# Latent attention: the order of key products, score tiles and the value sum within a step of TensorE

## The chip, the cores and the metric

One NeuronCore of a Trainium2 chip runs the whole program. The metric is the device time of one execution in microseconds, as the median of several runs.

## The reference

A decoder of two layers on x (2 x 1024 tokens, 256 channels). Each layer adds a self attention, a cross attention and a feed-forward block, each on the normalised x. Only the first block matters here, the latent attention of layer 0 (16 heads of 16 channels):

```python
latent_kv = (k + v) @ W_down_kv
k_rec, v_rec = latent_kv @ W_up_k, latent_kv @ W_up_v
scores = jnp.einsum('bhqd,bhkd->bhqk', qh, kh) * scale
decay = jnp.exp(-LAMBDA_DECAY * TIME_STEP * jnp.abs(idx[:, None] - idx[None, :]))
scores = scores * decay[None, None, :, :]
attn = jax.nn.softmax(scores, axis=-1)
out = jnp.einsum('bhqk,bhkd->bhqd', attn, vh)
```

(Clips, reshapes and the output projection are left out.) The softmax runs over all 1024 keys of a batch.

## The kernel before

The function `latent_attention` works in 16 groups of four heads and 512 queries (GROUPS), two groups for each set of heads. The products of queries and keys are needed twice, and are computed twice. First come the *score tiles* (`scores`, matmuls of line 653): 128 queries against 1024 keys of one head, 16 tiles a group, each in two of the PSUM banks 0 to 3. VectorE multiplies such a tile by the decay inside the diagonal block and takes each query's largest score (`highest`, line 814). When the 16 tiles of a group have been taken, GpSimd splits the peaks into three bf16 parts (`split_peaks`, lines 758 to 764), TensorE turns them into rows (`turn_peaks`, line 709), ScalarE copies the rows (`copy_peaks`, line 918) and SyncE stores them beside the stacked queries (line 623). So the peak is taken off within the matmul when the products come a second time: the *key products* (`key_scores`, line 660), 128 keys against 512 queries of one head, keys on the partitions, one bank each. ScalarE takes the exponential of each (`exponential`, line 913). In every second step the diagonal block has a *diagonal unit* of its own (`diagonal_scores`, four small matmuls, line 660 as well), and GpSimd selects the right side of the two (`select`, lines 772 and 775). The *value sum* (`sum_values`, lines 698 and 701) multiplies the probabilities of one key tile with the values of four heads in f32, four heads side by side in the columns of the array, and adds up in bank 7. When a group's eight key tiles are summed, ScalarE copies the sum (`copy_mix`, line 924), TensorE turns it (`turn_mix`, line 718), and VectorE divides by the sum of the weights (`weight`, lines 796 and 798).

A group has eight steps i, one for each key tile. What is interleaved in a step on TensorE is written out by hand in the loop of lines 725 to 739: the value sum of two steps ago, two key products, a score tile of the next group (tiles run ahead by LEAD = 6), two key products, a score tile; then `turn_peaks` of the next group if i is 5 (TURN_STEP), the diagonal unit if i is odd, `turn_mix` of the group before if i is 3. The score tiles end with step 4 of group 14, as then all groups have theirs.

Key products, the diagonal unit, and the results of both turns share three banks, 4 to 6, in a ring. The list `ring` holds all users in their order, each with the semaphore and the count that free it; `wait_for_bank` makes a user wait for the one three places ahead of it. For a key product that is its exponential; for `turn_mix` it is the weighting of its group by VectorE; for `turn_peaks` the copy of the rows. A score tile waits for VectorE to have taken the tile two before it (`peaked`).

VectorE has its own hand-written order (`run`, line 818), which must name tiles, units and weightings in TensorE's order. On the path without clips, which the profiled execution takes, a unit's step does nothing (`lambda g, i, h: None`), so VectorE's order is two tiles a step and, behind those of step 3, the weighting of the group before. ScalarE's queue has four exponentials a step, the mix copy of the group before behind the first one of step 1, the copy of the peak rows behind the fourth of step 5, and the diagonal unit's exponential at the end of odd steps.

Of the kernel before, what the change touches and what calls it, by code (L numbers as in the profile page):

```python
# [504 lines left out]
HEADS = 4  # L505
# [32 lines left out]
def latent_attention(k, v_heads, attn, decay, inner, stacks):  # L538
# [9 lines left out]
    GROUPS = 2 * B * H // HEADS  # L548
    TILES = HEADS * TPG
    LEAD = 6  # L550
    TURN_STEP = 5
# [6 lines left out]
    def on_diagonal(i):  # L558
        return i % 2 == 1

    def unit_index(g, i, h):

        return g * UNITS + i * HEADS + i // 2 + h
# [4 lines left out]
    def block_of(g, i):  # L568
        return key_tile(g, i) - g % 2 * TPG
# [17 lines left out]
    def bank_of(item):  # L587
        return 4 + place[item] % 3

    def wait_for_bank(pe, item):  # L590

        if place[item] >= 3:
            pe.wait_ge(*ring[place[item] - 3])

    with ExitStack() as c, nc.Block() as block:
# [16 lines left out]
        def tile_at(g, i, x):  # L612

            return (g + 1) * TILES + 2 * i + LEAD + x
# [25 lines left out]
        def _(pe):  # L640
            def scores(tile):

                g, x = divmod(tile, TILES)
                h, j = divmod(x, TPG)
                if x == 0:
                    stacks_arrived(pe, stacks, g)
                wait(pe, peaked, tile - 1)
                edge = (g % 2 * TPG + j + 1) * P
                for version in range(2):
                    for half in range(2):  # L650
                        lo, hi = max(half * G, 0 if version == 0 else edge), min((half + 1) * G, edge if version == 0 else S)
                        if lo < hi:
                            last = pe.matmul(k.ps[:, 2 * (tile % 2) + half, lo - half * G:hi - half * G],  # L653
                                             stacks.q[0:ROWS, g % 3, version, h, j * P:(j + 1) * P],
                                             stacks.k[0:ROWS, g // 2 % 2, version, h, lo:hi], start=True, stop=True)
                last.then_inc(scored, 1)

            def key_product(g, i, h, bank, version, lo, hi, at):
                kt = key_tile(g, i)
                return pe.matmul(k.ps[:, bank, at:at + hi - lo],  # L660
                                 stacks.k[0:ROWS + PARTS, g // 2 % 2, version, h, kt * P:(kt + 1) * P],
                                 stacks.q[0:ROWS + PARTS, g % 3, version, h, lo:hi], start=True, stop=True)

            def key_scores(g, i, h):

                item = (exp_done, unit_index(g, i, h) + 1)
                if i == 0 and h == 0:
                    pe.wait_ge(peaks_in, (g + 1) * 16)
                wait_for_bank(pe, item)
                edge = min(max(block_of(g, i) * P, 0), G)  # L670
                if edge > 0:
                    last = key_product(g, i, h, bank_of(item), 1, 0, edge, 0)
                if edge < G:
                    last = key_product(g, i, h, bank_of(item), 0, edge, G, edge)
                last.then_inc(key_scored, 1)

            def diagonal_scores(g, i):

                item = (exp_done, unit_index(g, i, HEADS) + 1)
                wait_for_bank(pe, item)  # L680
                lo = block_of(g, i) * P
                for h in range(HEADS):
                    last = key_product(g, i, h, bank_of(item), 1, lo, lo + P, h * P)
                last.then_inc(key_scored, 1)

            def sum_values(s):

                g, i = divmod(s, QT)
                n, kt = g // 2, key_tile(g, i)
                pe.wait_ge(exp_done, unit_index(g, i, HEADS if on_diagonal(i) else HEADS - 1) + 1)  # L690
                if i == 0:
                    pe.wait_ge(v_staged, n + 1)
                    wait(pe, mix_copied, g)
                if on_diagonal(i):
                    pe.wait_ge(selected, s // 2 + 1)
                    lo = block_of(g, i) * P
                    for h in range(HEADS):
                        pe.matmul(k.ps[VW * h:VW * (h + 1), PV_BANK, lo:lo + P], vh[:, n % 2, h, kt, :],
                                  probs_d[:, s // 2 % 2, h, :], start=False, stop=False, skip_group_check=True)
                for h in range(HEADS):  # L700
                    last = pe.matmul(k.ps[VW * h:VW * (h + 1), PV_BANK, :], vh[:, n % 2, h, kt, :], probs_of(s)[:, h, :],  # L701
                                     start=i == 0, stop=i == QT - 1, skip_group_check=True)
                last.then_inc(summed, 1)

            def turn_peaks(g):
                item = (peaks_copied, g + 1)
                pe.wait_ge(peaks_split, g + 1)
                wait_for_bank(pe, item)
                pe.matmul(k.ps[0:PARTS * 2 * TILES, bank_of(item), 0:P],
                          peak_parts[:, g % 2, :, :, :].rearrange("p r v t -> p (r v t)"),  # L710
                          ident_b[:, :], start=True, stop=True).then_inc(peaks_turned, 1)

            def turn_mix(g):
                item = (weighted, g + 1)
                pe.wait_ge(mix_copied, g + 1)
                wait_for_bank(pe, item)
                for j in range(TPG):
                    last = pe.transpose(k.ps[:, bank_of(item), j * P:(j + 1) * P], mix[:, g % 2, j * P:(j + 1) * P], k.ident[:, :])
                last.then_inc(mix_turned, 1)
# [4 lines left out]
                    turn_peaks(0)  # L724
            for g in range(GROUPS):
                for i in range(QT):
                    if g * QT + i >= 2:
                        sum_values(g * QT + i - 2)
                    for x in range(2):
                        for h in range(2 * x, 2 * x + 2):  # L730
                            key_scores(g, i, h)
                        if tile_at(g, i, x) < GROUPS * TILES:
                            scores(tile_at(g, i, x))
                    if i == TURN_STEP and g + 1 < GROUPS:
                        turn_peaks(g + 1)
                    if on_diagonal(i):
                        diagonal_scores(g, i)
                    if i == 3 and g > 0:
                        turn_mix(g - 1)
            for s in range(GROUPS * QT - 2, GROUPS * QT):  # L740
# [49 lines left out]
        def _(dve):  # L790
            def weight(g):
                b, first = divmod(g // 2 * HEADS, H)
                t = b * QT + g % 2 * TPG
                o = k.ps[:, bank_of((weighted, g + 1)), :].rearrange("p (j h d) -> p j h d", h=HEADS, d=VW)
                dve.wait_ge(mix_turned, g + 1)
                dve.reciprocal(inv[:, g % 2, :, :], o[:, :, :, HD]).then_inc(inverted, 1)
                dve.wait_ge(inverted, g + 1)
                dve.tensor_tensor(attn[:, t:t + TPG, first * HD:(first + HEADS) * HD].rearrange("p j (h d) -> p j h d", d=HD),
                                  o[:, :, :, 0:HD], inv[:, g % 2, :, :].unsqueeze(3).to_broadcast([P, TPG, HEADS, HD]),
                                  ALU.mult).then_inc(weighted, 1)  # L800
# [17 lines left out]
            def run(tile_step, unit_step, group_step):  # L818
                for tile in range(TILES + LEAD):
                    tile_step(tile)  # L820
                for g in range(GROUPS):
                    group_step(g)
                    for i in range(QT):
                        for x in range(2):
                            for h in range(2 * x, 2 * x + 2):
                                unit_step(g, i, h)
                            if tile_at(g, i, x) < GROUPS * TILES:
                                tile_step(tile_at(g, i, x))
                        if on_diagonal(i):
                            unit_step(g, i, HEADS)  # L830
                        if i == 3 and g > 0:
                            weight(g - 1)
                weight(GROUPS - 1)

            def clipped_path():
# [53 lines left out]

                own.did(dve.nop(nofuse=True))  # L890
                run(clipped_highest, clip_unit, spread_peaks)

            inside = dve.value_load(k.inside[0:1, 0:1], min_val=0, max_val=1)
# [1547 lines left out]
```

## Time and profile before

| | |
|---|---|
| median of three runs | 1449.26 us (1446.63 to 1449.71) |
| the profiled execution | 1447.3 us |
| its span | 1445.6 us |
| TensorE busy (matmul) | 1223.4 us, 85% of the span |
| VectorE, ScalarE busy | 798.4 and 763.2 us |

The latent attention's steps run from about 110 to 525 us of the span. All times in the rows further down are microseconds from the span's start. A row of the order of time merges instructions of one line that follow each other on an engine: start, length up to the last one's end, engine, line, operation, output and inputs, how many, and in brackets how long the engine had been idle and what ended that. Matmuls overlap in the array, so a row's length reaches past the next row's start; what a piece costs is the distance from its start to the next start. PE is TensorE's matmul, PEld its weight load, DVE VectorE, ACT ScalarE, POOL GpSimd.

### The profile page before, as it was taken

How to read it: one execution, taken by the hardware profiler on the slowest of the kernel's cores; microseconds unless marked ns; L12 is line 12 of the kernel's file. 1: busy time of each engine (PE TensorE's matmuls, PEld its weight loads, DVE VectorE, ACT ScalarE, POOL GpSimd, SP SyncE). 2: the span in 40 equal slices, each digit the busy share in tenths (PEclk: the TensorE clock that was granted, in tenths of full speed). 3: DMA queues.
4: the chain of work that ended last, by engine and by line, in shares of the span. 5: the costliest groups of instructions: out<-in, count | busy, mean ns of one | idle time of the engine just before them, and what ended most of it. 6: DMA issues, size and time to landing. Idle time of an engine off the chain costs nothing. (4 is left out here: it accounts for less than half of the span.)

```text
span 1445.6 us, 25437 instructions
## 1 busy us (share of the span) xinstructions
PE 1223.4 (85%) x8789; PEld 729.6 (50%) x8790; DVE 798.4 (55%) x1729; ACT 763.2 (53%) x1456; POOL 331.5 (23%) x567
## 2 busy tenths in 40 slices
PE   4869999999999987988456999878883799999992
PEld 2313444444444355435125552554362699999991
DVE  6977777777777427235777544572346322222223
ACT  3826777777777742663675668424632233333330
POOL 2922222222222211143520000211131222222220
PEclk9959999999999999999558999999996799999996
DMA  6770213321330003000001000051037111111115
GB/s 213 250 220 24 68 38 76 68 69 44 81 76 25 2 2 97 1 2 8 15 0 35 1 1 1 5 213 61 2 97 233 29 37 36 36 36 36 36 30 182
DMA packets 58656, 89.85 MB, mean 62 GB/s; under 512 B 10330, under 2 KB 48372, under 8 KB 56884
## 3 DMA queue, kind: packets, MB, share of 16 engines
q1 hardware_dynamic: 52694, 76.19, 17.7%
q0 software_dynamic: 3744, 10.23, 2.3%
q10 hardware_dynamic: 2112, 2.10, 0.4%
q8 instruction: 58, 0.95, 0.3%
q14 instruction: 48, 0.39, 0.1%
HBM read 66.21 MB, written 21.89 MB: 61 GB/s over the span
## 5 line engine op out<-in xcount | busy, mean ns | idle before, releaser
L814 DVE CUSTOM_DVE_ANT_0 faded_scores_sb<-banks,inner_sb 128x1024 f32<-128x1024 f32 x256 | 303.3, 1222 | 92.5 <-PE banks L653 91.4
L913 ACT ACTIVATE xt_sb<-banks 128x512 f32<-128x512 f32 x344 | 179.0, 605 | 72.2 <-PE banks L660 72.2
L660 PE MATMUL banks<-q_stack_sb,k_stack_sb 99*128 99x128 bf16 (+3 forms) x960 | 180.4, 296 | 5.9 <-ACT xt_sb L913 2.6
L653 PE MATMUL banks<-k_stack_sb,q_stack_sb 96*128 96x512 bf16 (+3 forms) x704 | 163.4, 338 | 7.2 <-DVE peak_sb L814 4.0
L660 PEld LDWEIGHTS banks<-q_stack_sb,k_stack_sb 99*128 99x128 bf16 x960 | 70.4, 97 | 159.9 <-ACT xt_sb L913 66.9
L2121 PEld LDWEIGHTS banks<-slots_xt_sb,attn_sb 128*128 128x128 f32 x1248 | 146.6, 193 | 1.9
L2121 PE MATMUL banks<-slots_xt_sb,attn_sb 128*128 128x128 f32 x1248 | 146.7, 276 | 0.0
L2133 PE MATMUL banks<-experts_w_sb,xt_sb 128*128 x624 | 141.2, 379 | 1.3 <-issue 1.3
L2133 PEld LDWEIGHTS banks<-experts_w_sb,xt_sb 128*128 128x128 f32 x624 | 115.5, 190 | 15.8 <-issue 1.7
L2173 ACT ACTIVATE slots_xt_sb<-banks 128x256 f32<-128x256 f32 x39 | 14.9, 383 | 177.5 <-PE banks L2107 177.5
L2230 DVE TENSOR_TENSOR slots_y_sb<-banks,tile_b_sb 128x256 f32<-128x256 f32 x39 | 16.6, 425 | 166.3 <-PE banks L2133 166.3
L913 ACT ACTIVATE probs_sb<-banks 128x512 f32<-128x512 f32 x168 | 87.3, 605 | 34.0 <-PE banks L660 34.0
L653 PEld LDWEIGHTS banks<-k_stack_sb,q_stack_sb 96*128 96x128 bf16 x704 | 65.8, 100 | 69.0 <-DVE peak_sb L814 17.9
L1227 DVE TENSOR_REDUCE peak_sb<-banks 128x8 f32<-128x616 f32 x64 | 49.9, 797 | 85.7 <-PE banks L1062 85.7
L701 PE MATMUL banks<-xt_sb,v_head_sb 128*32 128x512 f32 x688 | 90.6, 598 | 0.0
L252 POOL TENSOR_TENSOR x_sb<-x_sb,bb_sb 128x256 f32<-128x256 f32 x48 | 33.0, 731 | 244.9 <-DMA bb_sb<-in_L_attn_bo 193.8
L2183 ACT ACTIVATE xt_sb<-banks,tile_b_sb 128x128 f32<-128x128 f32 x312 | 84.7, 386 | 8.3 <-PE banks L2121 6.7
L1274 ACT ACTIVATE pt_sb<-banks,keyfill_sb 77x1024 f32<-77x1024 f32 x64 | 67.5, 1104 | 34.4 <-PE banks L1093 33.5
L2214 DVE COPY attn_sb<-experts_w_sb 128x2048 f32 x39 | 48.0, 1230 | 42.5 <-PE banks L2121 27.9
L2163 POOL DMA_INDIRECT outputs_y<-slots_y_sb,output_row_sb x39 | 39.6, 1015 | 127.5 <-DVE slots_y_sb L2230 127.5
L772 POOL TENSOR_SCALAR_AFFINE_SELECT xt_sb<-xt_sb 128x512 f32<-128x512 f32 x43 | 27.3, 635 | 180.8 <-ACT xt_sb L913 180.8
L2154 POOL DMA_INDIRECT slots_x_sb<-tokens_x,token_sb x39 | 38.2, 980 | 96.9 <-PE banks L2107 86.2
(316 smaller groups left out, 2017.0 us busy)
## 6 DMA issues: line engine op xcount, KB each, us to landing
experts_w_sb<-in_L_ffn_W SPq DMA_DIRECT2D x16, 1024.0 KB, 11.9
k_stack_sb<-k_parts SPq DMA_DIRECT2D x48, 256.0 KB, 4.9
q_stack_sb<-q_parts SPq DMA_DIRECT2D x96, 128.0 KB, 3.4
q_parts<-parts_sb SPq DMA_DIRECT2D x16, 384.0 KB, 2.6
k_parts<-parts_sb SPq DMA_DIRECT2D x16, 384.0 KB, 3.9
xt_sb<-outputs_y SPq DMA_DIRECT2D x8, 512.0 KB, 6.7
x_sb<-in_x SPq DMA_DIRECT2D x4, 512.0 KB, 5.6
w_raw_sb<-in_w_t SPq DMA_DIRECT2D x2, 1024.0 KB, 6.2
```

Of the source, the lines that this page charges most:

```text
L653: last = pe.matmul(k.ps[:, 2 * (tile % 2) + half, lo - half * G:hi - half * G], stacks.q[0:ROWS, g % 3, version, h, j * P:(j + 1) * P], st ...
L660: return pe.matmul(k.ps[:, bank, at:at + hi - lo], stacks.k[0:ROWS + PARTS, g // 2 % 2, version, h, kt * P:(kt + 1) * P], stacks.q[0:ROWS ...
L701: last = pe.matmul(k.ps[VW * h:VW * (h + 1), PV_BANK, :], vh[:, n % 2, h, kt, :], probs_of(s)[:, h, :], start=i == 0, stop=i == QT - 1, sk ...
L814: dve.tensor_tensor_reduce(out=junk[:, tile % 2, :], in0=tile_scores(tile), in1=inner[:, window(tile)], scale=1.0, scalar=-3.0e38, op0=ALU ...
L913: act.activation(out, k.ps[:, bank_of((exp_done, u + 1)), :], ACT.Exp).then_inc(exp_done, 1)
L1227: dve.tensor_reduce(peak[:, t % TPG, 2 * half:2 * half + 2, :], k.ps[:, bank:bank + 2, 0:SLOTS * C].rearrange("p r (s n) -> p r s n", n=C) ...
L1274: act.activation(pt[:, n % 2, 2 * half:2 * half + 2, :], k.ps[0:C, 2 * half:2 * half + 2, :], ACT.Exp, bias=key_fill[:, b:b + 1]).then_inc ...
L2121: last = pe.matmul(k.ps[:, 2 * u + f // HALF, (f % HALF) * P:(f % HALF + 1) * P], w1[:, u, kd, f * P:(f + 1) * P], xst[:, u, kd, :], start ...
L2133: last = pe.matmul(k.ps[:, 6, s * D:(s + 1) * D], ht[:, s, f, :], r.w2[:, bass.ds(e, 1), f, :].rearrange("p a n -> p (a n)"), start=f == 0 ...
L2163: pool.indirect_dma_start(out=scratch.y[:, :], out_offset=bass.IndirectOffsetOnAxis(ap=r.row[:, n:n + 1], axis=0), in_=ys[:, n % 2, :], in ...
L2183: ins = act.activation(ht[:, s, f, :], k.ps[:, 2 * s + f // HALF, (f % HALF) * P:(f % HALF + 1) * P], ACT.Gelu_apprx_tanh, bias=b1[:, s, f ...
L2214: dve.tensor_copy(w1[:, u, :, :].rearrange("p k n -> p (k n)"), r.w1[:, bass.ds(e, 1), :, :].rearrange("p a k n -> p (a k n)")).then_inc(c ...
```

## The change

The value sum moves behind the first two key products of a step. The third key product comes next, then the first score tile, then the fourth key product. `turn_peaks` (step 5) and the diagonal unit (odd steps) follow it directly, ahead of the second score tile, which is now the last of the step but for `turn_mix`. VectorE's order names the units and tiles in the same order.

```diff
             for g in range(GROUPS):
                 for i in range(QT):
+                    for h in range(2):
+                        key_scores(g, i, h)
                     if g * QT + i >= 2:
                         sum_values(g * QT + i - 2)
                     for x in range(2):
-                        for h in range(2 * x, 2 * x + 2):
-                            key_scores(g, i, h)
+                        key_scores(g, i, 2 + x)
+                        if x == 1:
+                            if i == TURN_STEP and g + 1 < GROUPS:
+                                turn_peaks(g + 1)
+                            if on_diagonal(i):
+                                diagonal_scores(g, i)
                         if tile_at(g, i, x) < GROUPS * TILES:
                             scores(tile_at(g, i, x))
-                    if i == TURN_STEP and g + 1 < GROUPS:
-                        turn_peaks(g + 1)
-                    if on_diagonal(i):
-                        diagonal_scores(g, i)
                     if i == 3 and g > 0:
                         turn_mix(g - 1)
...
                     for i in range(QT):
+                        for h in range(2):
+                            unit_step(g, i, h)
                         for x in range(2):
-                            for h in range(2 * x, 2 * x + 2):
-                                unit_step(g, i, h)
+                            unit_step(g, i, 2 + x)
+                            if x == 1 and on_diagonal(i):
+                                unit_step(g, i, HEADS)
                             if tile_at(g, i, x) < GROUPS * TILES:
                                 tile_step(tile_at(g, i, x))
-                        if on_diagonal(i):
-                            unit_step(g, i, HEADS)
                         if i == 3 and g > 0:
                             weight(g - 1)
```

## Rows read from the trace of the kernel before

**Rows 1.** Busy by stretch: length, engines' busy us, PEclk, DMA share, GB/s.

```profile
120.00:490.00 370.00, 367.45 (x2947) 151.79 (x2945) 281.40 (x488) 274.56 (x547) 87.01 (x181) 1.00 0.23 56
496.00:515.00 19.00, 16.50 (x132) 5.41 (x132) 0.68 (x2) 15.52 (x31) 3.89 (x7) 1.00 0.00 1
552.00:555.40 3.40, 3.40 (x18) 3.27 (x17) 3.29 (x12) 1.10 (x3) 0.00 (x0) 0.50 0.71 195
```

**Rows 2.** Order of time, TensorE: the value sums V(3) to V(7), V(0) to V(2).

```profile
300.06 0.43 PE L698 MATMUL banks<-probs_d_sb,v_head_sb 128*32 128x128 f32 x8
...
303.98 1.06 PE L701 MATMUL banks<-xt_sb,v_head_sb 128*32 128x512 f32 x8
...
306.82 0.43 PE L698 MATMUL banks<-probs_d_sb,v_head_sb 128*32 128x128 f32 x8
...
310.42 1.06 PE L701 MATMUL banks<-xt_sb,v_head_sb 128*32 128x512 f32 x8
...
313.26 0.42 PE L698 MATMUL banks<-probs_d_sb,v_head_sb 128*32 128x128 f32 x8
...
316.55 1.07 PE L701 MATMUL banks<-probs_sb,v_head_sb 128*32 128x512 f32 x8
...
319.38 0.42 PE L698 MATMUL banks<-probs_d_sb,v_head_sb 128*32 128x128 f32 x8
...
322.99 1.06 PE L701 MATMUL banks<-xt_sb,v_head_sb 128*32 128x512 f32 x8
```

**Rows 3.** Order of time, all engines: step 1 of a group, V(1) to D(1).

```profile
319.63 1.04 PE L701 MATMUL banks<-xt_sb,v_head_sb 128*32 128x512 f32 x8
...
320.60 0.11 PEld L660 LDWEIGHTS banks<-q_stack_sb,k_stack_sb 99*128 99x128 bf16 x2 [0.84 <-ACT xt_sb L913]
320.60 0.60 PE L660 MATMUL banks<-q_stack_sb,k_stack_sb 99*128 99x512 bf16 x2
...
321.03 0.60 ACT L913 ACTIVATE probs_sb<-banks 128x512 f32<-128x512 f32 x1 [0.99 <-PE banks L660]
...
321.52 0.59 ACT L924 ACTIVATE mix_sb<-banks 128x512 f32<-128x512 f32 x1
...
322.00 1.59 ACT L913 ACTIVATE probs_sb<-banks 128x512 f32<-128x512 f32 x3
322.66 0.23 PEld L660 LDWEIGHTS banks<-q_stack_sb,k_stack_sb 99*128 99x128 bf16 x4 [0.43 <-ACT probs_sb L913]
```

**Rows 4.** Order of time, all engines: S0(3), K0(4), weighting, S0(4), K2(4).

```profile
301.72 0.60 PE L653 MATMUL banks<-k_stack_sb,q_stack_sb 96*128 96x128 bf16 x3
...
304.98 0.60 PE L660 MATMUL banks<-q_stack_sb,k_stack_sb 99*128 99x512 bf16 x2
305.08 0.42 DVE L798 TENSOR_TENSOR attn_sb<-banks,inv_sb 128x256 f32<-128x256 f32 x1
...
305.42 0.60 PE L653 MATMUL banks<-k_stack_sb,q_stack_sb 96*128 96x384 bf16 x3
...
305.86 0.60 PE L660 MATMUL banks<-q_stack_sb,k_stack_sb 99*128 99x512 bf16 x2
```

**Rows 5.** Order of time, all engines: S0(4) and S1(4) on VectorE to D(5).

```profile
306.20 1.22 DVE L814 CUSTOM_DVE_ANT_0 faded_scores_sb<-banks,inner_sb 128x1024 f32<-128x1024 f32 x1 [0.69 <-PE banks L653]
...
307.35 1.22 DVE L814 CUSTOM_DVE_ANT_0 faded_scores_sb<-banks,inner_sb 128x1024 f32<-128x1024 f32 x1
...
308.46 2.06 ACT L913 ACTIVATE xt_sb<-banks 128x512 f32<-128x512 f32 x4 [0.99 <-PE banks L660]
...
309.36 0.60 PE L653 MATMUL banks<-k_stack_sb,q_stack_sb 96*128 96x512 bf16 x3
309.53 0.24 POOL L764 TENSOR_TENSOR peak_parts_sb<-peak_rest_sb,peak_parts_sb 128x32 bf16<-128x32 f32 x1
...
309.83 0.26 PE L709 MATMUL banks<-ident_b_sb,peak_parts_sb 128*96 128x128 bf16 x1
310.09 0.40 PE L660 MATMUL banks<-q_stack_sb,k_stack_sb 99*128 99x128 bf16 x4
```

## The prediction

> **What bounds the kernel now.** I read the page first for the engines and the granted clock, then the stretch of the latent attention alone, then the order of time of two steps, and last the places where TensorE starts something later than its own work allows. The change touches one stage only. In its 370 us from 120 to 490, TensorE is busy for 367.45 us at a granted clock of 1.00 (2.4 GHz), VectorE for 281 and ScalarE for 275 [rows 1]. So TensorE is the bound and the others have a quarter of their time free. But a busy TensorE can hide small waits, because the ends of matmuls are modelled, so I take the distances between starts.
>
> I call a step's pieces K0 to K3 (the key products, line 660), S0 and S1 (the two score tiles, 653), D (the diagonal unit, 660 x4), V (the value sum, 698 and 701), M (turn_mix, 718) and T (turn_peaks, 709). A number behind it in brackets is the step i of the group. From the starts [rows 2 to 4]: two K take 0.44, so one takes 0.22; an S takes 0.44; V takes 1.00 in an even step and 1.22 where line 698 comes with it; from D(1) to the V behind it are 0.33. An even step V to V is 2.84, and 1.00 + 4 x 0.22 + 2 x 0.44 is 2.76, with the rounding 0.09 over: what it costs to go over from bf16 products to V. So D is 0.33 - 0.09, or 0.23 rounded down. An odd step is 3.29, as step 7 shows: 1.22 + 0.88 + 0.88 + 0.23 + 0.09.
>
> The other step lengths [rows 2] tell where the order costs something now: step 3 takes 3.92, so M costs 0.63; step 5 takes 3.60, which is 0.31 over 3.29 (T and what waits about it); step 1 takes 3.61, 0.32 over. That last is a real wait: the mix copy stands in ScalarE's queue at 321.52 between two exponentials, and D(1) needs the bank of exp1 [rows 3]. The group is 2.84 x 4 + 3.29 + 3.92 + 3.60 + 3.61 = 25.8 us.
>
> **What the change does, part by part.** Nothing is added and nothing removed. TensorE's nominal work stays: V still follows bf16 work and is still followed by K, once a step, so the two changes of format stay too. On VectorE the order of real work is the same: its run takes the unmasked path (the custom operation of line 814 [rows 5]), on which the steps of units do nothing, so it still takes two tiles and, in step 3, the weighting. The list of banks has the order K0 K1 K2 K3 T D M before and after, so every wait has the value that it had. SyncE, GpSimd and ScalarE keep their queues. All that moves is *when*, within a step, TensorE comes to each wait. So I go through the waits.
>
> *K3 on exp0.* An exponential starts 0.43 after its product's start, lasts 0.60, and lets go some 0.06 later: 1.09 [rows 3]. K3 now comes 0.66 + 0.44 = 1.10 behind K0, just in time. It will come 1.09 + 0.22 + 0.44 later still. That is worth nothing where score tiles lie between. Where the tiles have run out (the last eleven steps), K3 waits 1.09 - 0.66 = 0.43 now; afterwards K1 waits for the exponential of the K2 or K3 three starts ahead of it, again 1.09 - 0.66. Nothing gained; I take 0, with 0.2 a step as bound on both sides, 2 us in all.
>
> *Step 1, the mix copy.* It waits for the last value sum of the group before, which is V(1). Count from V(1). V ends at 1.29 (319.63 + 1.04 less 319.38 [rows 2, 3]); the copy can start at about 1.34, exp1 at 0.48 behind it (1.82), and it lets go at 1.82 + 0.60 + 0.06 = 2.48. Now two key products, a tile and two more lie behind V and all that is waited for is D. Then D comes at 1.22 + 0.22 + 0.44 + 0.22 = 2.10 and waits 0.38. ScalarE goes on with exp2 at 2.30 and exp3 at 2.78, which lets go at 3.44; K1(2) comes at 2.48 + 0.23 + 0.44 + 0.22 = 3.37 and waits 0.07. V(2) is at 3.75 against 3.61: **+0.14**. Bounds: 0 (the copy starts as V's last pass ends) and 0.25.
>
> *Step 4, the weighting.* K2(4) takes the bank that M used, which VectorE frees with the weighting. VectorE can't do it earlier: in step 3 it has two tiles back to back. Now the weighting ends at 305.50, 3.78 behind S0(3), and K2(4) starts 4.14 behind it, so nothing waits [rows 4]. In the new order K2(4) is reached after S0 0.44, K3 0.22, D 0.23, S1 0.44, M 0.63, K0 and K1 0.44, V with its entry 1.09: 3.49. It must wait until 3.84: **+0.35**. Bounds: 0.2 (M dearer behind a tile than behind D) and 0.45.
>
> *Step 5, the turn of the peaks.* This is the dear one. T needs the peaks of the last tile of the next group, S1(4). The chain is: S0(4) at 305.42; VectorE takes it at 306.20 and S1(4) right behind at 307.35 (so S1's own time does not matter); GpSimd's four operations end at 309.77; T starts at 309.83, 4.41 behind S0(4) [rows 4, 5]. S1(5) had started at 309.36, so T waits 0.05 or less now: the chain is exactly covered. The new order puts T ahead of S1(5) and moves S0(4) later in its step as well. T is reached after S0(4) 0.44, K3 0.22, S1 0.44, K0 and K1 0.44, V with entry 0.09 + 1.22, K2 0.22, S0 0.44, K3 0.22: 3.73. It waits 0.68. In return D(5), which now starts 0.26 behind T because it waits for exp2 of its step (the third of the four in the row at 308.46, over at about 310.04), finds its bank free and follows at 0.06. Step 5 from V to V: 1.22 + 0.88 + 0.68 + 0.06 + 0.23 + 0.44 + 0.44 + 0.09 = 4.04 against 3.60: **+0.44**. Since K2(4) stands ahead of S0(4), its wait moves the whole chain and saves nothing here. Bounds: 0.25 and 0.6.
>
> *What could be late next.* T 0.4 later in the group brings the peak rows 0.8 nearer to the K0 of the next group that reads them: 6.9 us instead of 7.7, for one transfer; no row shows its landing, but no step 0 waits. I take 0; if that cover were gone it could cost up to 0.8 a group. The D of an odd step is ready long before; K1 behind it needs exp3 1.09 after K3 and comes 0.22 + 0.23 + 0.44 + 0.22 = 1.11 after: exactly enough, 0 to 0.03. S1 needs the banks of the step before's S1, off VectorE 0.78 + 1.15 x 2 = 3.1 behind that step's S0, and comes 2.84 + 0.66 = 3.5 behind it.
>
> **The sum.** The whole set of waits is in groups 1 to 13: 0.14 + 0.35 + 0.44 = 0.93 each, 12.1 us. Group 0 has no mix: 0.44. Group 14 has 0.49 and, without tiles behind T, about 0.1 in step 5. Group 15 has 0.14 in step 1, and in step 3 M runs beside exponentials that are waited for anyway: an estimate of -0.3. Together 12.9 us. The profiled execution took 1447.3 us (span 1445.6), 2.0 under the median of the three runs, 1449.26, and within their 1446.63 to 1449.71. So 1460.2 by the profile and 1462.2 by the median; I say 1461.
>
> **The rivals.**
> (1) *Weights loaded under V* (faster, 0.04). V costs 1.22 - 1.00 = 0.22 for 128 columns of each head, so 512 should cost 0.88 and not 1.00; 0.12 on leaving and 0.09 on entering are weight loads that nothing covers, 0.21 a step. The load of K0 behind V starts at 320.60, with its matmul, after 0.84 idle [rows 3]. If the new neighbours (K1 before, K2 behind, whose banks have been free for a microsecond) let these loads run ahead, 126 times 0.21 are 26 us back: 1461 - 26 = 1435. It decides from the first step without a wait. Against it: K0's bank was free as long, and it was late all the same.
> The Trainium skill, TensorE: Matmul & The Clock Gate, Part 2, step by step, says that the engine pulls weight loads ahead of running matmuls if their rows do not conflict or the spare weight buffer takes them. By that rule 1435 would be near; the trace agrees between K and S, and not behind V.
> (2) *The chain under T is shorter than I count* (no change, 0.05). If VectorE's two tiles or GpSimd's four operations took 0.7 less, T and the weighting would stay covered, and D(5) and D(1) decide: 1447 to 1450. The rows give no place for it.
> (3) *Half the waits* (0.03): 1455, if V's last pass and the weighting let go earlier than they end.
> (4) *The clock falls* (0.03). A stretch of 3.4 us at the lower level (0.50, 1.2 GHz) stands at 552 [rows 1]; in it TensorE does half its work, 1.7 us lost. One in each of 15 groups: +26, 1487. Against it: in the last steps, with TensorE busy 16.5 of 19 us, the clock stays at 1.00, and in the new order it will be busy for more than that.
> The same page, section on the second failure mode, says that small pauses between groups of matmuls that cycle through banks can make the clock swing. By it 1487 or more; the trace has such pauses in every group and shows no swing.
>
> **How the numbers follow.** Forecast 0.85, rivals 0.04, 0.05, 0.03, 0.03. The range takes the bounds of the three terms (0.45 to 1.3 a group, of which I leave out the outer quarters: 9 to 16 us), the 2 us of the last steps and the spread of the runs: 1455 to 1467. About 0.2%, 3 us, is what can be told from no change. Faster 0.04, same 0.05, slower 0.91.
>
> **What would show it.** In the new profile: steps of 4.04 (5), about 3.2 for V(4) to V(5), 3.75 (1), the rest as before; T held by GpSimd's line 764 for 0.7; a key product held by VectorE's line 798 in step 4. If T isn't held, the largest term is wrong; if even steps are shorter than 2.84, rival 1; if the clock row of the stage has anything but full, rival 4.

## The result, and the profile after

The changed kernel takes 1461.70 us (median of four runs, 1458.85 to 1462.95) against 1448.06 for the kernel before (four runs by now, 1446.63 to 1449.71): the ratio is 1.009, with a 95% interval of 1.0076 to 1.0105. It is slower by 13.6 us. The profiled executions took 1462.7 and 1447.3 us, with spans of 1460.9 and 1445.6.

The shortest view of where it went is the list of one line's instructions. The turn of the peaks T (line 709) comes once a group; the row gives how many there are, the shortest, median and longest in ns, and the first and last start in us. First the kernel before:

```profile
L709 PE MATMUL banks<-ident_b_sb,peak_parts_sb x16: 256/257/339, 107.0 to 490.2; 128*96 128x128 bf16 x16
```

and the changed kernel:

```profile
L709 PE MATMUL banks<-ident_b_sb,peak_parts_sb x16: 256/257/340, 107.3 to 505.8; 128*96 128x128 bf16 x16
```

From the first T to the last are 383.2 us before and 398.5 after. That is +15.3 us in 15 groups, 1.02 each. Ahead of the first T lie 107.0 and 107.3 us, behind the last 955.4 and 955.1: the sum of all the rest hardly moved. I use this distance, "T to T", for the runs below.

It needs a caution. The first T stands among the score tiles ahead of the first step, where the clock is low: from 105 to 115 us the granted clock is 0.50 in both kernels, from 115 to 125 us it is 0.99 before and 0.90 after. So T to T also holds what an edit puts behind the first T, and a piece at half speed. From the second T on the clock is full. In the same view from 120 us on, the second T starts at 129.5 us before and at 130.5 after, so from the second T to the last are 360.7 and 375.3 us: +14.6 in 14 groups, 1.04 each. Where an edit moves T to another step or changes the tiles that run ahead, only this second distance compares; a table further down has it for every run.

The busy time in nearly the same stretch as [rows 1], the changed kernel:

```profile
120.00:504.00 384.00, 367.05 (x2948) 153.84 (x2946) 283.69 (x488) 296.98 (x545) 86.88 (x177) 1.00 0.22 54
```

TensorE has done its 2948 matmuls with the same busy time (367.05 against 367.45 us for 2947), at the same full clock, but in 384 us instead of 370. The new time is waiting, not work. Who waited for whom, from 150 to 450, of the changed kernel (us in total, how many times, the longest):

```profile
PEld banks L660 <- DVE attn_sb L800: 16.3, 12, 1.4
...
PEld banks L709 <- POOL peak_parts_sb L766: 8.9, 11, 0.8
...
PE banks L709 <- POOL peak_parts_sb L766: 5.8, 11, 0.5
PE banks L660 <- DVE attn_sb L800: 5.5, 12, 0.5
```

In the same view of the kernel before TensorE's matmuls waited for nobody, and the weight loads of line 709 waited 2.5 us in all. Now a key product waits for VectorE's weighting (line 800) and T for GpSimd's last operation (line 766), once a group each. The steps, as the starts of the value sum V(1) to V(7), V(0) and V(1), in the order of time on TensorE:

```profile
301.56 0.43 PE L698 MATMUL banks<-probs_d_sb,v_head_sb 128*32 128x128 f32 x8
...
305.35 1.06 PE L701 MATMUL banks<-probs_sb,v_head_sb 128*32 128x512 f32 x8
...
308.19 0.43 PE L698 MATMUL banks<-probs_d_sb,v_head_sb 128*32 128x128 f32 x8
...
311.95 1.07 PE L701 MATMUL banks<-xt_sb,v_head_sb 128*32 128x512 f32 x8
...
315.32 0.43 PE L698 MATMUL banks<-probs_d_sb,v_head_sb 128*32 128x128 f32 x8
...
319.39 1.07 PE L701 MATMUL banks<-xt_sb,v_head_sb 128*32 128x512 f32 x8
...
322.23 0.43 PE L698 MATMUL banks<-probs_d_sb,v_head_sb 128*32 128x128 f32 x8
...
325.52 1.06 PE L701 MATMUL banks<-probs_sb,v_head_sb 128*32 128x512 f32 x8
...
328.36 0.43 PE L698 MATMUL banks<-probs_d_sb,v_head_sb 128*32 128x128 f32 x8
```

| step i, V to V, us | 1 | 2 | 3 | 4 | 5 | 6 | 7 | 0 | group |
|---|---|---|---|---|---|---|---|---|---|
| before [rows 2] | 3.61 | 2.84 | 3.92 | 2.84 | 3.60 | 2.84 | 3.29 | 2.84 | 25.8 |
| forecast | 3.75 | 2.84 | 3.92 | 3.19 | 4.04 | 2.84 | 3.29 | 2.84 | 26.7 |
| after | 3.79 | 2.84 | 3.76 | 3.37 | 4.07 | 2.84 | 3.29 | 2.84 | 26.8 |

And the two waits themselves in the order of time of all engines. The rows answer to those of [rows 4, 5]:

```profile
309.64 0.60 PE L653 MATMUL banks<-k_stack_sb,q_stack_sb 96*128 96x128 bf16 x3
...
310.51 0.60 PE L653 MATMUL banks<-k_stack_sb,q_stack_sb 96*128 96x256 bf16 x3
310.74 0.58 PEld L718 LDWEIGHTS banks<-ident_sb,mix_sb 128*128 128x128 f32 x4
310.95 0.60 PE L718 MATMUL banks<-ident_sb,mix_sb 128*128 128x128 f32 x4
...
312.99 0.42 DVE L800 TENSOR_TENSOR attn_sb<-banks,inv_sb 128x256 f32<-128x256 f32 x1
313.47 0.10 PEld L660 LDWEIGHTS banks<-q_stack_sb,k_stack_sb 99*128 99x128 bf16 x1 [1.36 <-DVE attn_sb L800]
313.47 0.39 PE L660 MATMUL banks<-q_stack_sb,k_stack_sb 99*128 99x512 bf16 x1 [0.45 <-DVE attn_sb L800]
...
313.70 0.60 PE L653 MATMUL banks<-k_stack_sb,q_stack_sb 96*128 96x384 bf16 x3
...
317.20 0.38 PE L660 MATMUL banks<-q_stack_sb,k_stack_sb 99*128 99x256 bf16 x2
...
317.81 0.24 POOL L766 TENSOR_TENSOR peak_parts_sb<-peak_rest_sb,peak_parts_sb 128x32 bf16<-128x32 f32 x1
...
318.11 0.26 PE L709 MATMUL banks<-ident_b_sb,peak_parts_sb 128*96 128x128 bf16 x1 [0.52 <-POOL peak_parts_sb L766]
...
318.20 0.39 PE L660 MATMUL banks<-q_stack_sb,k_stack_sb 99*128 99x128 bf16 x4
```

S0(3) starts at 309.64 and the weighting ends at 313.41, 3.77 behind it; S0(4) starts at 313.70 and T at 318.11, 4.41 behind it. Both chains have the length that they had before (3.78 and 4.41). TensorE arrives earlier and stands.

### The profile page after: what moved, and what is told of

The parts are those of the page before. It is cut to its first block and busy times, and to the rows that moved or that the text cites. A ratio compares the mean times of both kernels' runs of the same rounds, so it can differ in the third digit from the quotient of the medians.

```text
span 1460.9 us, 25437 instructions
## 1 busy us (share of the span) xinstructions
PE 1225.8 (84%) x8789; PEld 733.2 (50%) x8790; DVE 801.3 (55%) x1729; ACT 785.9 (54%) x1456; POOL 332.1 (23%) x567
## 5 line engine op out<-in xcount | busy, mean ns | idle before, releaser
L916 ACT ACTIVATE xt_sb<-banks 128x512 f32<-128x512 f32 x344 | 194.4, 602 | 56.1 <-PE banks L660 49.5
L660 PE MATMUL banks<-q_stack_sb,k_stack_sb 99*128 99x128 bf16 (+3 forms) x960 | 196.9, 298 | 12.5 <-DVE attn_sb L800 6.4
L660 PEld LDWEIGHTS banks<-q_stack_sb,k_stack_sb 99*128 99x128 bf16 x960 | 79.3, 98 | 172.8 <-ACT xt_sb L916 78.9
L916 ACT ACTIVATE probs_sb<-banks 128x512 f32<-128x512 f32 x168 | 95.2, 602 | 26.0 <-PE banks L660 22.7
```

The lines of the kernel that those rows point to most:

```text
L660: return pe.matmul(k.ps[:, bank, at:at + hi - lo], stacks.k[0:ROWS + PARTS, g // 2 % 2, version, h, kt * P:(kt + 1) * P], stacks.q[0:ROWS ...
L916: act.activation(out, k.ps[:, bank_of((exp_done, u + 1)), :], ACT.Exp).then_inc(exp_done, 1)
```

## The experiments

Theory A is that of the prediction: TensorE's work is unchanged, and three waits (step 1 for the mix copy, step 4 for the weighting, step 5 for the peaks) cost what TensorE arrives too early. Its rivals, in the expectations: B, that the place of V is itself the cost; C, that the place of T is; D, that the waits cover each other. The ratios are to the kernel before on the same chip, whose median was 1448.0 to 1448.4 us in these comparisons.

### One part of the change alone: V behind two key products

```diff
                     for x in range(2):
                         for h in range(2 * x, 2 * x + 2):
                             key_scores(g, i, h)
+                        if x == 0 and g * QT + i >= 2:
+                            sum_values(g * QT + i - 2)
```

(and the call ahead of the loop removed.)

> The kernel before with one part of the change alone: the value sum V stands behind the first two key products, all else as before (K0 K1 V S0 K2 K3 S1, then the turn of the peaks T, the diagonal unit D, the turn of the mix M). Theory A (the loss is made by T and by the bank of the weighting coming earlier than their chains allow): S0(4) to T is 0.44 + 0.44 + 0.44 + 0.44 + 1.31 + 0.44 + 0.44 + 0.44 = 4.39 us of TensorE's own work against a chain of 4.41, and K2(4) is 4.15 behind S0(3) against 3.84, so neither waits; only step 1 pays, as the mix copy still waits for V(1): 3.75 instead of 3.61 us. Total +0.14 x 15 = 2 us over the kernel before, some 1450. Theory B (where V stands is itself the cost: changes of format, weight loads, exponentials late behind V): most of the 13.6 us is there already, 1458 to 1462, and even steps are longer than 2.84.

Measured: 1457.39 us, ratio 1.0070 (1.0053 to 1.0087). T to T is 393.6:

```profile
L709 PE MATMUL banks<-ident_b_sb,peak_parts_sb x16: 256/257/342, 106.9 to 500.5; 128*96 128x128 bf16 x16
```

Even steps are 2.84, step 1 is 3.79, and T waits no more than before, as theory A says. But the expectation was wrong by 7 us, and most of the change's loss is there already: every odd step is longer, step 7 by 0.25 (3.54). The rows of one step 7, all engines:

```profile
321.28 1.09 ACT L913 ACTIVATE xt_sb<-banks 128x512 f32<-128x512 f32 x2 [0.99 <-PE banks L660]
...
321.73 1.08 PE L660 MATMUL banks<-q_stack_sb,k_stack_sb 99*128 99x128 bf16 x6
...
322.25 0.61 ACT L913 ACTIVATE probs_d_sb<-banks 128x512 f32<-128x512 f32 x1
...
322.41 0.10 PEld L660 LDWEIGHTS banks<-q_stack_sb,k_stack_sb 99*128 99x128 bf16 x1 [0.33 <-ACT xt_sb L913]
...
322.74 0.16 PEld L701 LDWEIGHTS banks<-probs_sb,v_head_sb 128*32 128x32 f32 x8 [0.23 <-issue]
```

K1 of the next step takes the bank of K3. With K2 and K3 back to back, ScalarE can start exp3 only 0.48 behind exp2 (the two in the row at 321.28), it ends at 322.37, and K1 loads at 322.41. In the changed kernel a score tile stands between K2 and K3. Then K3 follows exp2's start, its exponential is not queued, and by the prediction's count K1 is free 1.09 behind K3 and comes at 1.11; step 7 keeps its 3.29 there. So V's place does cost, through ScalarE's queue and the ring: B was half right, by a mechanism that I had only looked at for the full change. What the rest of the change gives and takes on top of it is in the steps: the spread takes away 0.25 in step 7, while T and D ahead of S1, and K2(4) reached early, cost 0.31 in step 5 and, with 3.76 + 3.37 against 4.03 + 2.84, 0.26 in steps 3 and 4.

### T and D back behind S1 in step 5

```diff
-                        if x == 1:
-                            if i == TURN_STEP and g + 1 < GROUPS:
-                                turn_peaks(g + 1)
-                            if on_diagonal(i):
-                                diagonal_scores(g, i)
+                        if x == 1 and i != TURN_STEP and on_diagonal(i):
+                            diagonal_scores(g, i)
                         if tile_at(g, i, x) < GROUPS * TILES:
                             scores(tile_at(g, i, x))
+                        if x == 1 and i == TURN_STEP:
+                            if g + 1 < GROUPS:
+                                turn_peaks(g + 1)
+                            diagonal_scores(g, i)
```

> The changed kernel with T and D of step 5 alone put back behind S1. Theory A: T is reached 0.44 later, of its wait of 0.52 to 0.68 us some 0.1 to 0.24 is left, step 5 goes from 4.07 back to 3.6 us, and 15 groups give 6.6 us: 1455. Steps 1 and 4 stay at 3.79 and 3.37. Theory B: step 5 keeps its length, the time stays at 1461.

Measured: 1461.06 us, ratio 1.0091 (1.0073 to 1.0110), as if nothing had been gained, where 1455 was expected. But T to T is 394.0, 4.5 us less than the changed kernel's (6.6 were expected):

```profile
L709 PE MATMUL banks<-ident_b_sb,peak_parts_sb x16: 257/257/340, 111.0 to 505.0; 128*96 128x128 bf16 x16
```

Its first T is at 111.0 instead of 107.3: this execution lost 3.7 us ahead of the attention, which the edit doesn't touch (more on that in the last section). Over the whole program the granted clock of this kernel's four executions is 0.914 to 0.917, that of the changed kernel's four 0.919 to 0.923. So the gain is shown by the trace and not by the median. Step 5 went from 4.07 to 3.73 and not to the expected 3.6, because another wait came up: K1(6) takes T's bank and T is now close ahead of it.

```profile
320.01 0.27 ACT L924 ACTIVATE peak_rows_sb<-banks 96x128 bf16<-96x128 f32 x1 [0.18 <-PE banks L709]
...
320.33 0.10 PEld L660 LDWEIGHTS banks<-q_stack_sb,k_stack_sb 99*128 99x128 bf16 x1 [0.25 <-ACT peak_rows_sb L924]
```

### The mix copy one place later in ScalarE's queue

```diff
-                        if i == 1 and h == 0 and g > 0:
+                        if i == 1 and h == 1 and g > 0:
                             copy_mix(g - 1)
```

> The changed kernel with the mix copy one place later in ScalarE's queue, behind exp1 of step 1 instead of exp0. Theory A: exp1 no longer waits for V(1), D(1) finds its bank free; the copy ends at 1.82 behind V(1), exp2 and exp3 let go at 2.48 and 2.96, K0(2) and K1(2) come at 2.77 and 2.99. Step 1 goes from 3.79 to 3.3 us, 15 times: 7.2 us, 1454.5. Theory B (ScalarE is not what holds D(1)): step 1 keeps 3.79.

Measured: 1455.23 us, ratio 1.0056 (1.0039 to 1.0072), where 1454.5 was expected. T to T is 391.5, 7.0 less than the changed kernel's, by 0.49 in step 1 (3.79 to 3.30):

```profile
L709 PE MATMUL banks<-ident_b_sb,peak_parts_sb x16: 257/257/343, 106.6 to 498.1; 128*96 128x128 bf16 x16
```

Theory A holds for step 1: 7.0 us of T to T for the 7.2 expected.

### The turn of the mix and the weighting ahead of S1(3)

```diff
                             if on_diagonal(i):
                                 diagonal_scores(g, i)
+                            if i == 3 and g > 0:
+                                turn_mix(g - 1)
...
                             if x == 1 and on_diagonal(i):
                                 unit_step(g, i, HEADS)
+                            if x == 1 and i == 3 and g > 0:
+                                weight(g - 1)
```

(and both calls at the end of step 3 removed.)

> The changed kernel with the turn of the mix M ahead of S1 in step 3, and VectorE's weighting accordingly ahead of its tile S1(3). Theory A: the weighting ends 2.64 behind S0(3) instead of 3.78, and K2(4), which comes at 3.5, waits for nothing; step 3 goes from 3.76 to 3.92 (M behind D's short matmuls is dearer), step 4 from 3.37 to 2.84: -0.37 in 14 groups, 5 us, 1456.5. Theory B: the wait of K2(4) isn't the bank's and moves elsewhere, 1461.

Measured: 1455.89 us, ratio 1.0061 (1.0045 to 1.0078), where 1456.5 was expected. T to T is 391.8, 6.7 less:

```profile
L709 PE MATMUL banks<-ident_b_sb,peak_parts_sb x16: 257/257/340, 107.1 to 498.9; 128*96 128x128 bf16 x16
```

Step 4 is 2.84 again and step 3 is 3.81: -0.47 a group, for which I had expected -0.37. The wait of K2(4) is that of the weighting's bank, and nothing took its place.

The 0.1 that I missed is in step 3: 3.92 was expected, as M stands behind D again. M takes the bank three places ahead of it in the ring, that of K2(3), and waits for its exponential. The end of that exponential and M's first weight load, in the kernel before:

```profile
302.68 0.60 ACT L913 ACTIVATE probs_sb<-banks 128x512 f32<-128x512 f32 x1
...
303.39 0.42 PEld L718 LDWEIGHTS banks<-ident_sb,mix_sb 128*128 128x128 f32 x4
```

and here:

```profile
306.71 0.60 ACT L916 ACTIVATE probs_sb<-banks 128x512 f32<-128x512 f32 x1 [0.67 <-PE banks L660]
...
307.43 0.31 PEld L718 LDWEIGHTS banks<-ident_sb,mix_sb 128*128 128x128 f32 x3
```

In both M loads 0.11 to 0.12 behind the exponential's end, and that holds in every group, though D's last matmul started 0.19 earlier in the one and only 0.09 in the other. So some of what M cost behind D was a wait for ScalarE.

### The chain to T begun a step earlier, and T a step later

```diff
-    LEAD = 6
+    LEAD = 8
```

> The changed kernel with LEAD 8 instead of 6: the score tiles run two further ahead, so the last tile of a group is S1(3) and the chain to the turn T (line 709) begins one step earlier. The order within a step is that of the change. Theory A (T is held by the chain tile, VectorE, GpSimd): T waits for nothing; D(5), 0.94 us behind K2(5), waits 0.15 for exp2; step 5 goes from 4.07 to 3.50, 8.5 us in 15 groups; two more tiles ahead of the first step cost 2 us, since VectorE takes one in 1.15. 1455. Theory C (T's place in the order is the cost, by its format or by what it does to the ring, not the chain): step 5 keeps 4.07, 1463.

Measured: 1455.18 us, ratio 1.0044 (1.0028 to 1.0060). Step 5 takes 3.49 with T where the change put it, ahead of D and S1. T to T is 391.7, 6.8 less, though the two tiles more lie inside it: from the first T to the first key product are 7.2 us instead of 4.7. From the second T to the last are 366.4, 8.9 less, for 8.5 expected. The whole row:

```profile
L709 PE MATMUL banks<-ident_b_sb,peak_parts_sb x16: 219/219/343, 106.7 to 498.4; 128*96 128x128 bf16 x16
```

The order is the change's, only the tiles are ahead, and the wait is gone: it is the chain and not the place, against theory C. D(5), behind T, waits for exp2 as expected (loads from the order of time on TensorE):

```profile
315.53 0.12 PEld L709 LDWEIGHTS banks<-ident_b_sb,peak_parts_sb 128*96 128x96 bf16 x1
315.83 0.23 PEld L660 LDWEIGHTS banks<-q_stack_sb,k_stack_sb 99*128 99x128 bf16 x4 [0.18 <-ACT xt_sb L916]
```

The other way to part the two is to turn later:

```diff
-    TURN_STEP = 5
+    TURN_STEP = 6
```

> The changed kernel with TURN_STEP 6 instead of 5: the turn T of the peaks (and GpSimd's split and ScalarE's copy with it) comes a step later. Theory A: T is reached 2.8 us later and never waits; step 5 is a plain odd step of 3.29, step 6 takes 2.84 + 0.06 + 0.15 (K1(7) comes 0.94 behind K3(6), whose exponential lets go at 1.09) = 3.05. Together 6.34 instead of 6.92, 8.7 us in 15 groups: 1453. If the peak rows then come too late for the next group's first key product, step 0 grows. Theory C: step 6 takes what step 5 loses, 1461.

Measured: 1455.17 us, ratio 1.0047 (1.0030 to 1.0064), where 1453 was expected. T to T is 395.0, but all T but the first come a step later, so it holds one step more; from the second T to the last are 369.0, 6.3 less than in the changed kernel. The profiled execution is the slowest of five, 1461.06 us, and its first T comes at 111.2. Steps 5 and 6 take 3.29 and 3.11, together 6.40 against 6.34 expected. The caution in the expectation came true in some groups: step 7 takes 3.50 there instead of 3.29. K0 of the next group waits for the DMA of the peak rows, as the waits from 150 to 450 say:

```profile
PEld banks L660 <- DMA q_stack_sb<-peak_rows_sb: 1.5, 5, 0.4
```

### One operation more in the chain

```diff
                 own.did(pool.tensor_copy(parts[1], peak_rest[:, :, :]))
                 own.wait()
+                own.did(pool.tensor_copy(parts[1], peak_rest[:, :, :]))
+                own.wait()
```

> The changed kernel with one cost put in: GpSimd's third operation of split_peaks is done twice, which makes the chain to the turn T longer by its 0.29 us. Theory A (in the changed kernel TensorE stands at T until the chain is over): all of it shows, step 5 goes from 4.07 to 4.36, 15 times: 4.4 us. Theory C (T's place, not the chain): 4.07.

> The kernel before with the same operation doubled. Theory A (in the kernel before the chain is covered to within 0.04, and D(5) behind T waits for exp2 until 310.09 anyway): T comes 0.29 later, at 310.12, D(5) 0.06 behind it at 310.18 instead of 310.09; step 5 goes from 3.60 to 3.70, 15 times: 1.4 us, a third of what the changed kernel pays for the same operation.

Measured: in the changed kernel 1466.63 us, ratio 1.0125 (1.0110 to 1.0139), T to T 402.3, +3.8; in the kernel before 1449.64 us, ratio 1.0009 (0.9999 to 1.0019), T to T 384.4, +1.2. The second interval holds 1: there the trace tells, and the median doesn't. Step 5 goes from 4.07 to 4.34 in the one and from 3.60 to 3.70 in the other. The changed kernel with the operation:

```profile
L709 PE MATMUL banks<-ident_b_sb,peak_parts_sb x16: 257/257/339, 108.2 to 510.5; 128*96 128x128 bf16 x16
```

and the kernel before with it:

```profile
L709 PE MATMUL banks<-ident_b_sb,peak_parts_sb x16: 257/257/342, 106.4 to 490.8; 128*96 128x128 bf16 x16
```

The same 0.3 us costs 0.27 a group where T is held and 0.10 where it is just covered. This is the direct measure of the prediction's main sentence, that the chain was exactly covered before and isn't now: D(5) had 0.2 to spare there, and only what goes beyond it shows.

### The kernel before with the mix copy later

The edit is that of the mix copy above, made in the kernel before.

> The kernel before with the mix copy behind exp1 instead of exp0 of step 1, nothing else. Theory A: the 0.31 us that D(1) waits in the kernel before come from the copy standing ahead of exp1: exp1 lets go 2.79 behind V(1), D(1) comes at 2.98. Step 1 goes from 3.60 to 3.29, 15 times: 4.7 us, 1443.5. Theory B: the wait moves on to K1(2) and stays: 1448.

Measured: 1444.16 us, ratio 0.9967 (0.9956 to 0.9979): faster than the kernel before by 0.3%. T to T is 380.0, 3.2 less; step 1 takes 3.36, where 3.29 was expected, against 3.60:

```profile
L709 PE MATMUL banks<-ident_b_sb,peak_parts_sb x16: 257/257/341, 108.7 to 488.7; 128*96 128x128 bf16 x16
```

The 0.07 that is left in step 1 is V(2), the first value sum of the next group. It starts bank 7 anew, and the kernel makes it wait for the mix copy (`mix_copied`), which now ends later. The copy and V(2):

```profile
296.60 0.61 ACT L924 ACTIVATE mix_sb<-banks 128x512 f32<-128x512 f32 x1
...
297.35 1.06 PE L701 MATMUL banks<-probs_sb,v_head_sb 128*32 128x512 f32 x8
```

D's last matmul starts at 297.12, so V follows it by 0.23. In the kernel before V follows D's last matmul by 0.15 (297.07 to 297.22).

### The changed order without its three waits

The edits of the mix copy, of the mix turn, and TURN_STEP 6:

> The changed order with the three waits taken away at once: mix copy behind exp1, mix turn and weighting ahead of S1(3), turn of the peaks in step 6. Theory A (the three waits are separate and add up): steps 0 to 7 are 2.84, 3.30, 2.84, 3.82, 2.84, 3.29, 3.05, 3.29, together 25.3 instead of 26.8 (and 25.8 in the kernel before): 1461.7 - 22 = 1440, under the kernel before by 8. Theory D (one wait covers another, since all three engines get later or earlier together): the gains of the single runs, 6.5, 5.8 and 8.7, do not add up, and the time stays at 1447 or above.

Measured: 1443.97 us, ratio 0.9966 (0.9951 to 0.9981), 4 us above the 1440 expected: steps 6 and 7 are 0.06 and 0.05 longer than expected (1.7 us in all), and the rest is open. The same with LEAD 8 and TURN_STEP 5:

> The changed order with mix copy behind exp1, mix turn and weighting ahead of S1(3), and LEAD 8 (the turn of the peaks stays in step 5). Theory A: steps 0 to 7 are 2.85, 3.30, 2.85, 3.82, 2.85, 3.49, 2.85, 3.29, together 25.3, with no step 7 of 3.5 as the later turn had; 2 us more ahead of the first step. 1442, under the kernel before by 6. Theory D (the gains do not add up): 1447 or more.

Measured: 1441.70 us for 1442 expected, ratio 0.9960 (0.9943 to 0.9978), the fastest of all kernels here, though its interval overlaps with the last two. T to T is 381.0 in the first, with one step more in it again, and 377.3 in the second. The first:

```profile
L709 PE MATMUL banks<-ident_b_sb,peak_parts_sb x16: 257/257/340, 108.7 to 489.7; 128*96 128x128 bf16 x16
```

and the second:

```profile
L709 PE MATMUL banks<-ident_b_sb,peak_parts_sb x16: 219/220/341, 107.4 to 484.7; 128*96 128x128 bf16 x16
```

From the second T to the last, in us (the changed kernel has 375.3):

| kernel | us | against the changed kernel |
|---|---|---|
| before | 360.7 | -14.6 |
| V alone behind two key products | 370.7 | -4.6 |
| T and D of step 5 back | 370.5 | -4.8 |
| mix copy later | 368.5 | -6.8 |
| mix turn and weighting earlier | 368.8 | -6.5 |
| LEAD 8 | 366.4 | -8.9 |
| TURN_STEP 6 | 369.0 | -6.3 |
| one operation more in the chain | 379.1 | +3.8 |
| before, one operation more | 362.1 | -13.2 |
| before, mix copy later | 357.5 | -17.8 |
| three edits with TURN_STEP 6 | 355.4 | -19.9 |
| three edits with LEAD 8 | 353.0 | -22.3 |

The three waits add up. Taken away one by one, the last by LEAD 8, they gave 6.8, 6.5 and 8.9 us, 22.2; taken away together 22.3. With TURN_STEP 6 for the last it is 19.6 and 19.9. Theory D falls. The steps of the last kernel are 3.30, 2.85, 3.81, 2.85, 3.49, 2.85, 3.29, 2.84, 25.28 a group, 0.5 under the kernel before. So the spread order as such is not what made it slow, but what it was put into: a ScalarE queue, a place of the weighting and a lead of tiles that fit the old order. That it is better than the old order is not shown. The old order got only the first of the three edits, and gained 0.24 a group by it; with all three it was not run.

## Why the prediction was right, point by point

1461 us was forecast and 1461.70 measured; slower was given 0.91.

*TensorE's work is the same, only waits move.* Right: the even steps are 2.84, steps 7 and 0 as before, the busy time is equal.

*Step 1, +0.14.* Measured +0.18. D(1) comes 304.05 - 301.56 = 2.49 behind V(1), by this row of the changed kernel's TensorE (2.48 was forecast):

```profile
304.05 0.40 PE L660 MATMUL banks<-q_stack_sb,k_stack_sb 99*128 99x128 bf16 x4 [0.23 <-ACT xt_sb L916]
```

The rest is K1(2), which waits about 0.09 and not 0.07.

*Step 4, +0.35.* The term was right as a sum and wrong in its parts. K2(4) waits 0.53 and not 0.35, as it gets there earlier, and step 3 is shorter by 0.16: M costs 0.44 behind a tile where it cost 0.63 behind D. The mis-sized term is M. The prediction took its 0.63 for M's own cost and gave its wait for a bank no term, though in the kernel before M loads 0.11 behind the end of exp2(3), the exponential of K2(3), in every group; in the new order S1 covers that. My bounds named only a dearer M behind a tile, and it got cheaper. It did not matter because the wait ends with the weighting, 3.77 behind S0(3), whatever lies between. Steps 3 and 4 together were forecast at 7.11 and take 7.13.

*Step 5, +0.44.* Measured +0.47. The chain is 4.41 as read; TensorE gets to T at about 317.42 (317.20 + 0.22) and waits 0.69, against 0.68; D follows at 0.09 instead of 0.06. The experiments show it by three routes: the tiles earlier, the turn later, the chain longer.

*The D that waited before.* Right: D(5) has no wait of its own any more, and the operation added to the chain of the kernel before cost 0.10, as the 0.2 that D(5) had to spare there says.

*The sum.* The set of waits is 1.04 a group and not 0.93: 0.04 more in step 1, 0.03 in step 5, 0.02 in steps 3 and 4 together, and the rest in hundredths of the other steps. T to T grew by 15.3, for which the forecast had 13.1 (its 12.9 has -0.16 behind the last T). The medians are 13.6 apart, the profiled pair 15.4. Both lie inside the range. That 1461 and 1461.70 are less than 1 us apart is in part luck: the stage lost 2 us more than forecast, and the spread of the runs, some 4 us from lowest to highest in the changed kernel, gave it back in the median.

*The rivals.* Weights loaded under V: no. The load behind V still starts with its matmul, after 0.84 idle, in the changed kernel (and so does that of a score tile, where V alone was moved: 320.41, after 0.84 too):

```profile
316.53 0.11 PEld L660 LDWEIGHTS banks<-q_stack_sb,k_stack_sb 99*128 99x128 bf16 x2 [0.84 <-ACT xt_sb L916]
```

By the rule of the Trainium skill (TensorE: Matmul & The Clock Gate, Part 2, step by step) on loads that are pulled ahead it should have started earlier; the trace shows this rule for M (its f32 load at 310.74 lies under S1(3), which began at 310.51), and not behind V, where 32-column tiles are in flight. The clock: 1.00 from 120 to 504 us, with about 15 us more of waiting in it; the swing that the Trainium skill describes for kernels that cycle through banks (same page, the second failure mode) did not come.

*What wasn't foreseen* was in an expectation: V alone behind two key products, 2 us forecast and 9 measured. That K3's exponential frees K1 with "exactly enough" time was worked out for the change only and not for the part of it.

## What to carry to other kernels

When the bound engine walks through an order written by hand, list for each of its waits the chain that ends it and the anchor where that chain begins, and count both ways from the anchor: the engine's own work, and the chain. A reordering costs, for each wait, what the engine gets there too early, and here these sums, made from one trace, came within a few hundredths of a microsecond a step. They have to be made anew for each order: the one for V alone left out a wait of 0.25 a step and missed by 7 us. If the new order is wanted, move the other engines' queues with it (here the copy, the weighting and the lead), or it is judged by waits that aren't its own.

## What the runs showed of the hardware

The time ahead of the attention differs between executions of the same code there: the first T is at 106.4 to 108.7 us in eleven profiled kernels and at 111.0 and 111.2 in two. The granted clock in the stretch from 29 to 39 us is 0.51 and 0.53 in those two and 0.84 to 1.00 in the eleven. The kernel before, and the one with T and D put back:

```profile
29.00:39.00 10.00, 9.32 (x25) 3.45 (x23) 5.90 (x15) 6.40 (x13) 5.67 (x6) 1.00 0.44 157
```

```profile
29.00:39.00 10.00, 9.32 (x12) 2.16 (x10) 3.84 (x9) 3.07 (x5) 4.32 (x4) 0.51 0.36 126
```

At 0.51, near the lower level of 1.2 GHz, TensorE gets through 12 matmuls where it gets through 25 at 2.4 GHz, with the same busy time, 9.32 us. From 19 to 29 us it had been as busy in both, 6.96 and 6.90 us; what made the clock fall in one is open. A difference of 4 us between two executions can come from this alone, which is why the distances between the T were the better measure.

M's first f32 weight load (0.14 us) is hidden under S1's last matmul in the changed kernel: it starts at 310.74, M's first matmul at 310.95. Where M stands behind D it starts 0.11 behind the end of the exponential that frees M's bank, whatever the distance to D, so those runs don't show what D's short matmuls would hide of it.
